# Moving projections and large transfers by two steps, and a new order of pairs and context matmuls, in a fused RWKV and graph-attention kernel

## The reference, cut to what matters

```python
for c in range(6):
    nsrc = min(c + 1, 5); snode = c - nsrc
    q = ew[c, 0] * (nodes[c - 1] @ We[eq] + be[eq])
    k = ew[c, 1] * (nodes[snode] @ We[ek] + be[ek])
    v = ew[c, 2] * (nodes[snode + nsrc // 2] @ We[ev] + be[ev])
    o = mha(q, k, v, Wq[c], Wk[c], Wv[c], Wo[c])   # softmax(q k^T / 4) v per head
    nodes[c] = act_w[c] * o + q
out = layernorm(nodes[5])                          # and x2 + out is returned
```

## Time and profile before

| | us |
|---|---|
| median of 3 runs | 2377.87 (2376.58 to 2405.42) |
| profiled execution | 2382.87, its span 2381.0 |
| TensorE busy | 2247.4 (94%), 16493 matmuls |
| VectorE busy | 2069.2 (87%) |
| ScalarE busy | 1795.6 (75%) |
| GpSimd busy | 529.2 (22%) |
| mean granted TensorE clock | 0.971 |
| tiles of maxima, of 1536 | 628 whole, 908 in halves |

### The profile page before, as it was taken

The page is one execution under the profiler, slowest core; times in us unless marked ns, Lnnn a source line. Parts: engine busy times, 40 slices in busy tenths (PEclk is TensorE's granted clock), DMA queues, the critical chain, the costliest instruction groups (busy, mean ns, idle before and its releaser), DMA issues.

```text
span 2381.0 us, 43523 instructions
## 1 busy us (share of the span) xinstructions
PE 2247.4 (94%) x16493; PEld 905.9 (38%) x16493; DVE 2069.2 (87%) x3260; ACT 1795.6 (75%) x3432; POOL 529.2 (22%) x667
## 2 busy tenths in 40 slices
PE   7998999999999999999999999999999999999998
PEld 3533333343333333343333333333333333334333
DVE  6878899898999988998988988989889879889896
ACT  4366787787787877887877877878778778778776
POOL 4330320222312202212202112112022022321213
PEclk9989999999999999999999999999999999999999
DMA  4230322323314314224223223134033132331301
GB/s 130 57 64 21 78 58 57 78 59 71 76 38 91 66 34 87 56 60 87 57 49 79 62 54 76 35 73 85 23 79 74 32 80 52 71 76 44 66 24 50
DMA packets 87535, 149.37 MB, mean 63 GB/s; under 512 B 35146, under 2 KB 49950, under 8 KB 87326
## 3 DMA queue, kind: packets, MB, share of 16 engines
q0 software_dynamic: 28224, 94.13, 18.9%
q1 hardware_dynamic: 59102, 52.46, 8.8%
HBM read 42.36 MB, written 14.91 MB: 24 GB/s over the span
## 4 chain that ended last, share of the span: by engine, by line
PE 69%; DVE 17%; DMA 10%; issue 2%; SPq 1%; ACT 1%; POOL 0%; DVEq 0%; POOLq 0%; ACTq 0%
PE context L646 26%; PE ring L601 24%; DMA rows_dram<-max_turn 8%; PE wide L625 8%; DVE max_neg L1234 8%; DVE max_neg L1231 6%; PE wide L527 2%; PE wide L516 2%; PE wide L508 2%; DMA q_aug<-rows_dram 2%; PE wide L536 1%; PE wide L541 1%; PE context L471 1%; DVE max_all L1240 1%; DVE max_part L1245 1%
## 5 line engine op out<-in xcount | busy, mean ns | idle before, releaser
L877 ACT ACTIVATE e_ring<-ring 128x512 f32<-128x512 f32 x3054 | 1603.2, 600 | 421.6 <-PE ring L601 419.7
L1231 DVE TENSOR_REDUCE max_neg<-wide 128x1 f32<-128x512 f32 x1816 | 1145.2, 682 | 184.6 <-PE wide L625 183.6
L625 PE MATMUL wide<-k_aug,q_aug 48*128 48x512 f32 x3072 | 1089.1, 448 | 42.0 <-DVE max_neg L1231 33.1
L601 PE MATMUL ring<-q_aug,k_aug 50*128 50x512 f32 x3054 | 1048.5, 441 | 57.8 <-DMA q_aug<-rows_dram 56.3
L646 PE MATMUL context<-e_ring,v_aug 128*32 128x256 f32 (+1 forms) x9168 | 922.9, 475 | 0.6 <-ACT raw L886 0.6
L1234 DVE TENSOR_REDUCE max_neg<-wide 128x2 f32<-128x1024 f32 x628 | 762.3, 1218 | 59.4 <-PE wide L625 58.5
L601 PEld LDWEIGHTS ring<-q_aug,k_aug 50*128 50x128 f32 x3054 | 501.7, 189 | 773.4 <-ACT e_ring L877 593.9
L625 PEld LDWEIGHTS wide<-k_aug,q_aug 48*128 48x128 f32 x3072 | 508.7, 188 | 95.8 <-DVE max_neg L1231 64.1
L646 PEld LDWEIGHTS context<-e_ring,v_aug 128*32 128x32 f32 x9168 | 182.1, 109 | 417.9 <-issue 281.4
L381 POOL DMA_DIRECT2D src<-node_dram x40 | 22.9, 571 | 719.2 <-PE wide L527 719.2
L1335 POOL CAST q_part<-q_part 128x512 fp32r<-128x512 f32 x46 | 28.1, 611 | 453.6 <-ACT q_part L846 440.0
(11 more groups left out here) (240 smaller groups left out, 957.5 us busy)
## 6 DMA issues: line engine op xcount, KB each, us to landing
q_aug<-q_part POOLq DMA_DIRECT2D x138, 256.0 KB, 4.7
k_aug<-k_part POOLq DMA_DIRECT2D x138, 256.0 KB, 7.1
src<-node_dram POOLq DMA_DIRECT2D x40, 512.0 KB, 7.0
ctxT<-raw SPq DMA_DIRECT2D x380, 32.0 KB, 2.0
rden_bc<-rden_dram SPq DMA_DIRECT2D x23, 512.0 KB
node_dram<-node_ring SPq DMA_DIRECT2D x16, 512.0 KB, 2.9
q_aug<-rows_dram SPq DMA_DIRECT2D x192, 8.0 KB
node_ring<-in_L_attn_x SPq DMA_DIRECT2D x4, 512.0 KB, 4.9
```

Of the source, the lines that this page charges most:

```text
L601: e.matmul(bk[:, :], k_aug[first:first + AUG, u % 2, h // 2, chunk * P:(chunk + 1) * P].bitcast(F32R), q_aug[first:first + AUG, u % 2, h / ...
L625: e.matmul(bk[:, :], q_aug[first:first + SPLIT, u % 2, head // 2, q0:q0 + P].bitcast(F32R), k_aug[first:first + SPLIT, u % 2, head // 2, h ...
L877: e.activation(e_ring[:, n % E_SLOTS, :], bank[where["st", n]][:, :], ACT.Exp, scale=EXP_SCALE).then_inc(a_exp, 1)
L1231: e.tensor_reduce(max_neg[:, G % 2, kh, row:row + 1], wide[:, b, :], AX_X, ALU.max, negate=True).then_inc(v_mx, 1)
```

## The change

It has five parts, all in the schedule; what is computed stays the same.

- In units after the first the products move two steps on: K to r = 7 and 11 (from 5 and 9), out to 15 and 19 (13, 17), turn to 21 (19), V to 23 and 27 (21, 25), Q to 31 and 3 of the next unit (29, 1). Units 0 and the last keep the old places.
- Q moves go from r = 3..8 to 5..10. K moves go from r = 10, 11 to r = 12, 13, and wait for d_rows, the store of the rows of r = 12. The first source load goes from r = 26 to r = 28 and waits the same way. normalise goes from r = 8 to 10, the reciprocals from the end of r = 3 to the start of r = 8, their store and spread from 4, 5 to 8, 9, the spill of a node from 19 to 21. V is evicted before the maxima of the step after its product.
- In two steps without a product TensorE does pairs 0, 1, 2; context columns 256 (z = s-2) and 128 (z = s-1); two pairs; 384 columns; three pairs; 256 columns. Before it was 2 pairs, 256, 3 pairs, 512, 3 pairs, 256, which stays where there are products.
- From tile 88 on three of four tiles go in halves (w % 4 != 3); before it was every second.
- In unit 0 TensorE goes step by step: two pairs, the products, 256 columns, two pairs, 256 columns, then the slice of the first part. Its products take ring banks, and ScalarE evicts them after the second exponential.

```diff
-        K_AT, OUT_AT, TURN_AT, V_AT, Q_AT = (5, 9), (13, 17), 19, (21, 25), (29, UC + 1)
+        K_AT, OUT_AT, TURN_AT, V_AT, Q_AT = (7, 11), (15, 19), 21, (23, 27), (31, UC + 3)
+        FIRST_K_AT, FIRST_V_AT, FIRST_Q_AT, LAST_OUT_AT, LAST_TURN_AT = (5, 9), (21, 25), (2, 3), (13, 17), 19
@@ q_steps
-            return (first + Q_AT[0], first + Q_AT[1]), first + UC + 3
+            return (first + Q_AT[0], first + Q_AT[1]), first + UC + 5
@@ bank of each maxima matmul
-            if s >= 0 and s % 2 == 1:
+            if s >= UC and s % 2 == 1:
                 taken += len(products(s))
@@ in_halves
-            return w >= SPLIT_FROM and w % 2 == 0 or MAX_BANK_OF[2 * w] > MAX_BANK_OF[2 * w + 1]
+            return w >= SPLIT_FROM and w % 4 != 3 or MAX_BANK_OF[2 * w] > MAX_BANK_OF[2 * w + 1]
@@ TensorE
-            for s in range(0, ALONE, 2):
+            for s in range(0, UC):
+                made = products(s)
                 pair(s, 0)
                 pair(s, 1)
-                if s > 0:
-                    weighted(s - 2, second_half, False, True)
+                for kind, unit, hf in made:
+                    product(kind, unit, hf, next_bank())
+                if s > 0 and not made:
+                    weighted(s - 1, first_half, True, False)
                 pair(s, 2)
                 pair(s, 3)
+                if made:
+                    weighted(s - 1, whole, True, True)
+                elif s > 0:
+                    weighted(s - 1, second_half, False, True)
+                mix_at(s)
+
+            for s in range(UC, ALONE, 2):
+                pair(s, 0)
+                pair(s, 1)
+                made = products(s + 1)
+                if not made:
+                    pair(s, 2)
+                if s > UC:
+                    weighted(s - 2, second_half, False, True)
+                if made:
+                    pair(s, 2)
+                else:
+                    weighted(s - 1, slice(0, BANK // 4), True, False)
+                pair(s, 3)
                 pair(s + 1, 0)
-                if s > 0:
+                if made:
                     weighted(s - 1, whole, True, True)
+                else:
+                    weighted(s - 1, slice(BANK // 4, BANK), False, True)
                 mix_at(s)
                 pair(s + 1, 1)
                 pair(s + 1, 2)
                 pair(s + 1, 3)
@@ VectorE
+            def before_maxima(s):
+
+                u, r = divmod(s, UC)
+                nxt, prev = u + 1, u - 1
+                if 1 < nxt < UNITS and r - 1 in V_AT:
+                    evict_v(nxt, V_AT.index(r - 1))
+                if 0 <= prev < LAST and r == 8:
...
+                    e.reciprocal(rden_pack[:, :], den_pack[:, :]).then_inc(v_rec, 1)
@@ POOL
+            def wait_rows_stored(s):
+
+                for G in finished(s):
+                    e.wait_ge(d_rows[G % 2], DMA * (G // 2 + 1))
+
-                    if r == 26:
+                    if r == 28:
+                        wait_rows_stored(s)
                         load_source(e, nxt + 1, 0)
-                if 0 <= prev < LAST and (r, half) == (8, 1):
+                if 0 <= prev < LAST and (r, half) == (10, 1):
                     normalise(prev)
-                    if r == 10:
-                        e.wait_ge(p_st, HG * s)
+                    if r == 12:
+                        wait_rows_stored(s)
                         for n in range(K_MOVES // 2):
                             move_k(e, nxt, n)
-                if 1 <= nxt < UNITS and half == 0 and r == 11:
+                if 1 <= nxt < UNITS and half == 0 and r == 13:
@@ SP
-                        if r == 4:
+                        if r == 8:
                             store_rden(prev)
-                        if r == 5:
+                        if r == 9:
                             spread_rden(prev)
-                        if r == 19 and CELLS[prev][0] < SPILLED:
+                        if r == 21 and CELLS[prev][0] < SPILLED:
                             spill(prev)
```

64 lines of the change are left out of this document (39 added, 25 removed).

## The result

The changed kernel takes 2257.74 us (median of 4 runs, 2253.71 to 2262.4) against 2383.81 for the kernel before (4 runs, 2376.58 to 2405.42). The ratio is 0.9458, 95% interval 0.939 to 0.9525: faster by 5.4%. The forecast was 2237 us, with a range of 2195 to 2300. The profiled execution took 2258.64 us, its span 2256.8; the profiled span of before was 2381.0, so 124.2 us went.

What follows compares the result with a forecast made beforehand. TensorE, busy 1960.65 of 2054.37 us in units 1 to 22, was taken as the bound, each micro-stall counting. Terms summed to -141: 2382.87 profiled became 2241.9, and the median, 5.0 lower, 2237 us; range 2195 to 2300.

Steps and rivals of the forecast that it cites:

- K moves and source loads behind the rows: Units 1 to 22: large transfers no longer hold the row store, removing idle and low-clock time; -94 us, bounds -50 to -101.
- products two steps later: Two-steps at r = 4, 12, 20, 28 become bare, so the closing-work stall goes; -66 us, bounds 0 and -75.
- 3, 2, 3 pairs: Bare two-steps: a fourth set of weights (0.07 us) and ring pressure (0.03) cost +18 us, bounds 0 to +44.
- halves: VectorE's tiles: 0.06 us more for each of some 270 changed tiles, none on the path; term 0.
- SP late at r = 20: SP's row store leaves at +5.9, giving a new wait of 0.4 us a unit; +9 us, bounds 0 to +22.
- unit 0: Step by step again: more changes between pairs and columns, but fewer half-clock stretches; -8 us, bounds -20 to +10.
- unit 23 and tail: Last unit: it has few products and keeps its stalls; term 0.
- control by unit 9: Unit 9: K moves and source load issued after the store, read 1.98 us behind it, two-step stayed at 4.59 us.
- Rival 1: Row store or reads stay late, half to all of the 94 us remains; 2284 to 2331 us, chance 0.14.
- rival 3: SP becomes late at r = 20, each unit losing 5 + 2 us; 2391 us, chance 0.05.
- Rival 2: The closing-work stall stays because VectorE is near full in bare two-steps; 2303 us, chance 0.10.
- rival 4: Better: no new SP wait, no cost of the fourth set, unit 0 at its good end; 2198 us, chance 0.06.

Runs made afterwards that it cites:

- E11: The changed kernel with only the products, and the reciprocals, normalise and Q moves that depend on them, back at the old steps; 2270.04 us, ratio 0.9527.
- E1: The kernel before with only the K moves (r = 12, 13) and first source load (r = 28) waiting for the stored rows; 2289.97 us, ratio 0.9616.
- E3: The changed kernel with the old order of pairs and columns in every two-step; 2244.25 us, ratio 0.9408.
- E4: The changed kernel with the old rule for tiles, every second one in halves; 2263.47 us, ratio 0.9498.
- E7: The changed kernel with SP's context moves of a unit's first two groups behind the row store of r = 20, units 1 to 22; 2235.27 us, ratio 0.9368.
- E2: The changed kernel without the two waits for the stored rows, the first source load back at r = 26; 2256.0 us, ratio 0.947.
- E9: E2 with the reciprocals, their store and spread, and normalise back at r = 4, 4, 5 and 8; 2251.43 us, ratio 0.944.
- E6: The changed kernel with VectorE's mixing pieces in units 1 to 6 moved off the two-steps that close a group; 2243.93 us, ratio 0.9407.
- E12: E8, but with the early reciprocals, their transfers and normalise only for the last unit; 2220.24 us, ratio 0.9284.
- E8: The changed kernel with E3, E7 and E6 together, reciprocals at r = 6, their transfers at 6 and 7, normalise at r = 9; 2223.33 us, ratio 0.9329.

## Why the prediction was right, and where its steps were off

The working was made against 2382.87 us and gave 141 off; the span fell by 124.2. Term by term (units 1 to 22 unless said; the line for the products is what remains after the others; E11, with the SP wait that goes with it added, puts it at 17.9 + 18.6 = 36.5 us):

| term of the prediction | forecast | measured | from |
|---|---|---|---|
| K moves and source loads behind the rows | -94 | -95.6 | E1 |
| products two steps later | -66 | -44.2 | remainder |
| 3, 2, 3 pairs | +18 | +13.5 | E3 |
| halves | 0 | -8.1 | E4 |
| SP late at r = 20 | +9 | +18.6 | E7 |
| unit 0 | -8 | -15.6 | windows |
| unit 23 and tail | 0 | +5.4 | windows |
| start of step 0 | 0 | +1.8 | 101.48 and 103.27 |
| sum | -141 | -124.2 | |

So 17 us of the miss of 21 are in the sum. The rest, 4, is the step from the profiled execution to the median: 5.0 forecast, 0.9 here. That the sum is no further off is partly luck: the products, SP and unit 23 came out worse than forecast by 36.8 us, the halves and unit 0 better by 15.7.

**K moves and source loads: right in size, one mechanism of it not as told.** E1 gives the 94 us, in the two places and nearly in the shares of the working. "The rows' reads now leave together with the K moves" is so in E1 and not in the changed kernel, where POOL's own order holds the moves 6 us behind the store (E2). The kernel would do as well without the new wait at r = 12 (E2), and without normalise's new place besides: in E9 the later K product alone leaves the moves 2.57 us behind the store. Each arrangement is enough, and together they hide each other. The control by unit 9 was a good one, though "nothing else differs" passed over its first K move, which did stand ahead of the store (E1). Rival 1 did not come.

**Products two steps later: nearly right per unit, wrong over all units.** For units 7 to 22 the remainder is 106.7 - 77.7 (E1) + 6.6 (E3) - 4.6 (E4) + 17.4 (E7) = 48.4 us of gain. The 4.4 us at r = 24 of units 11 and 22 stand in E3 and in E7, so 44.0 is nearer, 2.75 per unit, and E11 gives 2.7; "22 x (3.3 - 0.3)" had 3.0. What failed is the 22. In units 1 to 6 the same sum gives a loss of 4.3, where 18 us of gain were forecast: a difference of 22 us, as much as the whole miss. Two things stand there that the step did not look at. Pieces of the first part lay at the half steps 4.5, 12.5 and 29.5, so they now share a bare two-step, 4.6 us long, with the closing work; moving them gave 7.8 us (E6). And normalise moved with the products from r = 8 to r = 10. There it waits for the spread denominators until r = 12 has begun, and starts beside the joining of the maxima (E9). The prediction listed normalise's move in no term. The argument was made on units 9 and 14 and multiplied by 22; units 1 to 6, whose steps hold other work, were never looked at.

**3, 2, 3: the size came near by luck (13.5 for 18), the mechanism failed.** It was to cost 0.10 us in every bare two-step, 0.07 for the fourth set of weights and 0.03 for the ring. In quiet units the bare two-steps sum to 37.2 us with either order, so both prices are near nothing there. What E3 gave came from loaded units and from two low-clock stretches that are not the order's (E3).

**Halves: the term 0 was mis-sized.** Its cost was looked at and its gain was not. The likely gain is the bank that comes free half a tile earlier, which the earlier trace rows showed (0.6 and 1.14 us).

**SP: the right mechanism, half the size.** The store was to leave at +5.9 and left at +6.7; a wait of 0.4 us was to follow and it was 0.8 (16.5 us in 20 waits). Low clock behind the two longest waits, 4.4 us in units 11 and 22, was not in the term (E7). This is rival 3 at a small scale: 1.1 us a unit and not 7, with waits of 0.35 to 2.00 us where rival 3 had 5, and a fall of the clock behind two of them and not behind each. Its 2391 us lay inside the band that the prediction called "same", 2330 to 2425. The mark set for it, "over 1 us at r = 24", was too low: unit 14 has 1.2 and rival 3 was not the case.

**Unit 0** gave 15.6, inside its bounds of -20 to +10. How much of it is the clock and how much the even spacing of the tiles is not told apart.

**Unit 23 and tail** were put at nothing because their products stay. They still changed, since the order of pairs, the halves and the places of the reciprocals and of normalise apply there too. Two windows of the last unit of the changed kernel, r = 8 and r = 12:

```profile
2172.26:2177.43 5.17, 5.17 (x52) 2.29 (x48) 5.17 (x9) 4.61 (x10) 0.00 (x0) 1.00 0.03 6
2182.50:2193.20 10.70, 8.62 (x49) 3.21 (x46) 8.16 (x12) 5.23 (x11) 2.37 (x1) 0.84 0.02 5
```

and the same of the kernel before:

```profile
2300.68:2305.34 4.66, 4.66 (x44) 1.90 (x41) 4.66 (x7) 4.46 (x10) 2.25 (x1) 1.00 0.06 14
2310.02:2317.38 7.36, 7.07 (x49) 2.78 (x45) 6.31 (x11) 5.24 (x11) 0.00 (x0) 1.00 0.03 7
```

In the changed kernel VectorE is busy all of the 5.17, and no product two-step stands between to give it time back; the two-step from r = 12 holds the third of the long joining instructions. With normalise earlier the rest falls to 102.4 (E9), with the old order besides to 100.6 (E12).

**What the profile was to show** came for the marks on r = 16, on the closing two-steps (4.60 to 4.72), on the maxima waits (10.7 us in 13 waits, under 15) and on the clock, 1.00 in units 7 to 22 but 0.98 in units 1 to 6. Rival 2 did not come; of rival 4 only unit 0 at its good end did.

Open: the rest of units 1 to 6. In E12 they are still 542.7 - 6 x 84.7 = 34 us above the quiet units, of which the work of the first part itself, the two meetings (1.1 and 1.2 us beside E8) and unit 6 are not told apart.

## What to carry to other kernels

A gain worked out on one clean stretch holds for the stretches that carry the same work; before it is multiplied, look at what else sits at the same place of the cycle in the others, on every engine. When work is moved, list what moves with it: here a GpSimd operation that slid along into VectorE's tightest spot cost 4 to 5 us in each of two units. A term that comes out near its forecast can still be wrong in every place: compare the places too, not only the sum. And when several arrangements each keep large transfers behind a small urgent one, test each alone, since any of them may be idle.
